# Turning gathered token rows by DMA instead of on the matmul engine, in a graph network with a mixture of experts on one core

## What is computed

```python
x = x + gnn(layernorm(x))     # h = silu(x @ W_in.T + b_in), then h + term_1 + ... + term_6,
                              # term_i = mean over edges of term_(i-1), divided by i; then @ W_out.T + b_out
x = x + moe(layernorm(x))     # 3125 tokens x 256
# moe: 8 experts, each token goes to its 2 best, softmax weights
for e in range(E):
    h = gelu(einsum('bsd,dh->bsh', xn, W1[e]) + b1[e], approximate=False)    # 256 -> 512
    y = y + (einsum('bsh,hd->bsd', h, W2[e]) + b2[e]) * w_full[..., e, None]  # 512 -> 256
```

## Time and profile before

| | |
|---|---|
| Three runs | 1204.22, 1207.3, 1209.26 us; median 1207.3 |
| The profiled execution | 1203.97 us, of which the span of the trace is 1202.2 |
| TensorE clock granted, mean over the span | 0.987 of full |
| Busy in the span | PE 95%, DVE 58%, ACT 35%, POOL 19% |
| Graph part, to the last matmul of line 2059 | to about 1004.5 us |
| Expert tiles, first matmul of line 2173 to last of line 2187 | 1006.4 to 1183.7 us |

### The profile page before, as it was taken

How to read it: one execution, slowest core, us unless ns; L and a number is a source line. 1 busy time by engine, 2 the same in 40 slices (tenths; PEclk the granted TensorE clock), 3 DMA queues, 4 the chain that set the end, 5 groups by cost and what they waited for, 6 DMA issues and landing times.

```text
span 1202.2 us, 26290 instructions
## 1 busy us (share of the span) xinstructions
PE 1143.5 (95%) x7856; PEld 810.2 (67%) x7856; DVE 700.4 (58%) x1425; ACT 418.6 (35%) x806; POOL 227.3 (19%) x279
## 2 busy tenths in 40 slices
PE   5798999999999999999999999999999999899993
PEld 3586777776566666666666666666666667799993
DVE  7898999994444433443155433443344586775666
ACT  1676656663100000000022102121122236677682
POOL 2000000000012121112100000000112236567762
PEclk8998999999999999999999999999999999999997
DMA  6111011013344424443334303331224323323377
GB/s 158 57 43 39 27 32 31 26 34 103 87 92 93 90 56 105 102 100 71 66 114 126 100 23 114 97 109 61 33 66 146 119 84 124 91 79 99 116 211 203
DMA packets 77196, 105.98 MB, mean 88 GB/s; under 512 B 13559, under 2 KB 62510, under 8 KB 76988
## 3 DMA queue, kind: packets, MB, share of 16 engines
q1 hardware_dynamic: 63997, 75.26, 21.0%
q0 software_dynamic: 11376, 25.55, 9.4%
q10 hardware_dynamic: 1740, 4.11, 1.4%
HBM read 77.00 MB, written 37.49 MB: 95 GB/s over the span
## 4 chain that ended last, share of the span: by engine, by line
PE 83%; DVE 9%; DMA 2%; issue 2%; ACT 2%; DVEq 1%; ACTq 0%; POOL 0%; SPq 0%; POOLq 0%
PE ps L2005 45%; PE ps L2059 11%; PE ps L1983 7%; PE ps L2173 5%; PE ps L1951 5%; PE ps L2187 5%; DVE v_b L1244 3%; PE ps L1919 1%; DMA h_ring<-h_dram 1%; PE ps L1930 1%; DVE adj L1151 1%; PE ps L2087 1%; PE ps L2107 1%; ACT v_b L1089 1%; DMA adj<-y_dram 0%
## 5 line engine op out<-in xcount | busy, mean ns | idle before, releaser
L2005 PE MATMUL ps<-v_a,adj 125*125 125x512 f16 x1375 | 297.3, 379 | 0.0
L2005 PE MATMUL ps<-v_b,adj 125*125 125x512 f16 x1250 | 270.2, 379 | 1.5 <-DVE v_b L1269 1.5
L2005 PEld LDWEIGHTS ps<-v_a,adj 125*125 (+1 forms) x1375 | 187.6, 136 | 109.0
L2005 PEld LDWEIGHTS ps<-v_b,adj 125*125 x1250 | 170.6, 136 | 100.9 <-issue 2.0
L964 ACT ACTIVATE t_hi<-ps,cinv 125x256 f32<-125x256 f32 x125 | 59.2, 474 | 457.0 <-PE ps L2005 404.0
L1251 DVE SCALAR_TENSOR_TENSOR t_hi<-ps,cinv,t_hi 125x256 f32<-125x256 f32 x125 | 60.3, 483 | 240.7 <-ACT t_hi L964 240.7
L1244 DVE TENSOR_TENSOR v_b<-v_b 125x2560 f16<-125x2560 f16 x125 | 180.2, 1487 | 3.4 <-PE ps L1951 2.9
L2059 PE MATMUL ps<-v_b,adj 125*125 125x512 f16 x625 | 139.8, 380 | 0.3 <-issue 0.3
L939 ACT ACTIVATE adj<-ps 125x625 f32 (+1 forms) x125 | 112.1, 906 | 66.0 <-PE ps L1951 65.0
L1983 PE MATMUL ps<-v_a,adj 125*125 125x512 f16 x500 | 123.4, 378 | 0.0
L2059 PEld LDWEIGHTS ps<-v_b,adj 125*125 125x125 f16 x625 | 83.4, 137 | 46.2 <-issue 0.7
(11 more groups left out here) (282 smaller groups left out, 986.2 us busy)
## 6 DMA issues: line engine op xcount, KB each, us to landing
h_ring<-h_dram SPq DMA_DIRECT2D x125, 125.0 KB
v_a<-L_ffn_W SPq DMA_DIRECT2D x32, 256.0 KB, 3.4
v_b<-L_ffn_W SPq DMA_DIRECT2D x32, 256.0 KB, 3.4
adj<-w_dram SPq DMA_DIRECT2D x16, 512.0 KB, 5.3
adj<-y_dram SPq DMA_DIRECT2D x8, 560.0 KB
w_dram<-w_hi SPq DMA_DIRECT2D x32, 128.0 KB, 1.9
hx_dram<-h_dram POOLq DMA_DIRECT2D x25, 125.0 KB, 2.4
hx_dram<-x POOLq DMA_DIRECT2D x25, 125.0 KB, 3.2
```

Of the source, the lines that this page charges most:

```text
L2005: last = te.matmul(ps[0:NP, u, :], of_tile(adj[0:NP, 0:ADJ], i, u, a * NP, NP), source[:, a, :], start=(a == 0), stop=(a == T - 1))
```

## The change

- The four transposing matmuls of each tile and ACT's copy out of PSUM are gone. SP issues one transposing DMA a tile instead, from `x_g[j % 8]` straight to `xT16[j % 4]`. It waits for the gather and for `hidden(j-4)`, and PE's `hidden(j)` waits for the DMA. A gather waits for the DMA of the tile eight before.
- Tiles 0 and 1 are turned in SP's last loop pass, before that pass stores its row tile (18); they wait until PE has read `vb[:, 0:4, :]` for the last time (`v_read`). Row tiles 19 to 24 are stored after the transfers of tiles 3 and 9 to 13.
- The loads of lots 0 to 2 go from SP to ACT, behind tiles 42, 43 and 44; ACT waits there for the scatters of tiles 0 to 36. SP's `store(0)` comes just after tile 53 is turned, the other stores and loads after tile 55.
- `HH_TILES` becomes 3 to 16 and 47 to 55 (was 6 to 16 and 44 to 55); 23 tiles in both.

```diff
-    HH_TILES = [*range(6, 17), *range(44, FT)]
+    HH_TILES = [*range(3, 17), *range(47, FT)]
-        TURN_AT = (T - 10, T - 5)
+        LOADS_AT = (42, 43, 44)
 (sync, in the last step's body)
+                if m == T - 1:
+                    sp.wait_ge(S["v_read"], 1)
+                    turned(0)
+                    turned(1)
                 if has(6):
                     rows_out(m - 6, (u - 6) % WIN)
+            def turned(j):
+                sp.wait_ge(g_in[j % FU], 16 * (j // FU + 1))
+                need(sp, S["ffn_h"], j - XR + 1)
+                sp.dma_start_transpose(xT16[j % XR], x_g[j % FU]).then_inc(x_turned[j % XR], 16)
-            for w in range(T - 6, T):
-                rows_out(w, w % WIN)
-            sp.wait_ge(S["tok_ps"], 2)
-            sp.wait_ge(S["idx_ok"], 2)
-            landed(0)
-            for n in range(3):
-                for k in range(TOP):
-                    load(n, k)
-            store(0)
+            for j in range(2, FT):
+                turned(j)
+                if j == XR - 1:
+                    rows_out(T - 6, (T - 6) % WIN)
+                if 9 <= j < 9 + WIN:
+                    rows_out(T - WIN + j - 9, j - 9)
+                if j == FT - 3:
+                    store(0)
             store(1)
 (gpsimd, gather)
-                    pool.wait_ge(S["xg_T"], j - FU + 1)
+                    pool.wait_ge(x_turned[(j - FU) % XR], 16 * ((j - FU) // XR + 1))
 (scalar: transposed(j) and its calls go; in between(j))
+                if j == LOADS_AT[0]:
+                    for r in range(FY):
+                        act.wait_ge(y_out[r], scattered(CLASS_TILES[0], r))
+                if j in LOADS_AT:
+                    n = LOADS_AT.index(j)
+                    t0, t1 = LOTS[n]
+                    for k in range(TOP):
+                        for part in HALVES:
+                            act.dma_start(y_in[n][k][part], y_v[k, part, t0:t1, :]).then_inc(yc_in[n], 16)
 (tensor: transposed(j) and its calls go)
-                        if m == T - 1 and a in TURN_AT:
-                            transposed(TURN_AT.index(a))
+                        if m == T - 1 and a == XR - 1:
+                            last.then_inc(S["v_read"], 1)
 (tensor, hidden)
-                    if j < LAG:
-                        pe.wait_ge(S["xgT_ok"], j + 1)
+                    pe.wait_ge(x_turned[j % XR], 16 * (j // XR + 1))
 (tensor, result)
-                if b == 0 and not alone:
-                    pe.wait_ge(S["xgT_ok"], j + LAG + 1)
```

More of the change, by code:

```diff
@@ L397, in gnn_ffn @@
             pool_turn cover_sum cover_ps cover_ok term_ok e_const e_in e_col e_oh e_mm e_acc e_read e_term e_rows
-            xg_T xgT_ok ffn_h gelu_ok hh_ok hs_ok ffn_y y_ok comb_ok""".split()
+            v_read ffn_h gelu_ok hh_ok hs_ok ffn_y y_ok comb_ok""".split()
         S = {n: sem(n) for n in names}
@@ L406, in gnn_ffn @@
         g_in = [sem(f"g_in{r}") for r in range(FU)]
+        x_turned = [sem(f"turned{r}") for r in range(XR)]
         y_out = [sem(f"y_out{r}") for r in range(FY)]
@@ L432, in turned_in @@
             return [w for w in range(T) if turn_slot(w) == m]
-        def turn_bank(j):
-            return 2 if j == 0 else (j - 1) % 2
         def rows_place(w):
@@ L1023, in body @@
                     normalised(m - 5, u, i)
-                if m == T - 1:
-                    transposed(0)
-                    transposed(1)
                 if has(0):
@@ L1046, in root_of @@
                 a.activation(sd2[:, 0:count], ve2[:, 0:count], ACT.Sqrt).then_inc(S["sd_ok"], 1)
[L1048 to L1053, removed]
             def column(row, w):
@@ L1119, in _ @@
                 if j == 0:
-                    transposed(2)
                     transposed_rows(T - 1)
-                if j + LAG < FT:
-                    transposed(j + LAG)
                 between(j)
@@ L1849, in weighted @@
                     done.then_inc(S["comb_ok"], 1)
-            def transposed(j):
-                pass
             def hidden(j, b, e, part):
@@ L1876, in tables_ready @@
                 pass
-            ffn_tiles(dve, FT, FA, LAG, (experts, parts), 1, transposed, hidden, result, between, tables_ready)
+            ffn_tiles(dve, FT, FA, LAG, (experts, parts), 1, hidden, result, between, tables_ready)
             for n in range(3, len(LOTS)):
@@ L2076, in body @@
                     positions(7, POS_AT, planes_a, oh_pos_a, (0, GA), True, True, 0).then_inc(S["tok_ps"], 1)
[L2078 to L2088, removed]
             def transposed_rows(w):
@@ L2195, in _, with ffn_tiles @@
             pe.wait_ge(S["w_in"], 16 * 2 * NE)
-            ffn_tiles(pe, FT, FA, LAG, (parts,), HK, transposed, hidden, result, between, tables_ready, addresses)
-def ffn_tiles(eng, count, second, lag, tables, steps, transposed, hidden, result, between, tables_ready, addresses=None):
+            ffn_tiles(pe, FT, FA, LAG, (parts,), HK, hidden, result, between, tables_ready, addresses)
+def ffn_tiles(eng, count, second, lag, tables, steps, hidden, result, between, tables_ready, addresses=None):
     entries = {0: [load(0, eng) for load in tables]}
@@ L2208, in ffn_tiles @@
                 result(j - lag, b, *entries[j - lag], alone=j >= count)
-            if b == 0 and 0 < j < count - 2:
-                transposed(j + 2)
             if j < count:
                 hidden(j, b, *entries[j])
-            if b == steps - 1 and j == 0:
-                transposed(2)
             if b == 0 and j + 1 < count and j + 1 != second:
```

## The result

Four runs of the changed kernel took 1218.86, 1218.96, 1219.0 and 1227.47 us, median 1218.98, against 1205.76 for the kernel before (four runs, 1203.66 to 1209.26): **ratio 1.0113, 95% interval 1.0092 to 1.0134, slower by 1.1%**. The forecast was 1197 us, with a range from 1190 to 1208. The profiled execution took 1218.96 us.

A forecast was written before the change was run, and what follows sets the result against it. PE was taken to bound the expert stage, ACT second, DVE early. Terms -12.3 - 1 + 1 + 1 + 1 = -10.3 us on the profiled 1203.97 gave 1193.7, or 1197 against the median 1207.3; range 1190 to 1208.

The forecast's parts named there:

- Point 8: Lot loads' burst from 1140 us: gather and transposing DMA, 7 us each, against 15.9 us less POOL's 2.7; stall 1, bounds 0-6.
- Point 1: PE in the expert stage: 56 groups of transposing matmuls at 0.22 us go, gaining 12.3 us; tile 2.87 to 2.65 us.
- the longer figure weighed beside it: The Trainium skill's about 275 ns per PE transposing matmul, against 55 ns by the rows; 61.6 us gain instead of 12.3.
- Points 3 and 4: DVE-paced first tiles: 1.5 us kept, 1 us more gained; tiles 9 to 16: 1 us taken back; each bounds 0 and 2.
- Point 7: Start of the expert stage: tile 0's transposing DMA lands about 1004.7, PE needs it at 1006.0; cover 1.3 us, cost nothing.
- Point 5: ACT behind tiles 42 to 44: four load issues a lot at 496 ns; 1 us of stall, bounds 0 and 2.6.
- Point 6: Transposing DMA in steady state: 3 us to landing, under 2.65 us of queue time a tile, 8 us cover; cost nothing.
- the slower rival: Expert stage: transposing DMAs do not keep the pitch, a tile takes 3.2 us; 1214 to 1247 us; chance 0.12.

The follow-up runs named there:

- e3: Changed kernel with the twelve loads of lots 0 to 2 cut by max_dma_last_dim=256 into packets of about 256 bytes: 1256.0 us, 1.0112.
- e8: Changed kernel with the loads on SP's queue, close together behind tiles 46, 47 and 48: 1250.98 us, 1.0062.
- e11: Changed kernel with the loads of lots 0 to 2 in pieces of at most 1024 bytes: 1250.47 us, 1.0047.
- e1: Changed kernel without the 12 loads of lots 0 to 2: 1243.25 us, 0.9989 of the kernel before.
- e16: Changed kernel without the loads of lots 0 to 2, a second time: 1246.5 us, 1.0012 of the kernel before.
- e5: The changed kernel as it is, run again beside variants on a later chip: 1.0086 of the kernel before.
- e15: The changed kernel as it is, run again in the last group: 1.0077 of the kernel before.
- e4: Kernel before, turning on PE, with only the loads of lots 0 to 2 moved to ACT behind tiles 42 to 44: 1246.56 us, 1.0023.
- e9: Exact copy of the kernel before, run for its profile on a later chip: 1242.02 us, 0.9979.
- e10: Kernel before, turning on PE, with thirty transposing DMAs added for tiles 12 to 41 into an unread buffer: 1246.31 us, 1.0017.
- the spread version: Changed kernel with the loads four tiles apart: on ACT behind tiles 42, 46, 50, 1.0024 and 1.0053; on SP behind 46, 50, 54, 1.0006 and 1.0016.

## Why the prediction was wrong

**Point 8, the burst, is the step that failed.** It held a gather and a transposing DMA of 7 us each, 14 together, against a cover of some 13, and allowed 1 us of stall, at most 6. Measured for tile 48 were 10.0 and 18.2 us, 28.2 together, and PE waited 13.7 us before tiles 47 and 48. I had taken the scatters' 7.0 us, 1 KB pieces on their own queue, for a transfer in 256-byte packets, while the earlier trace rows had the loads' size: 3.84 MB in 924 packets, 4.2 KB each. Whether the size of the packets is what makes the difference stays argued (e3, e8 and e11). And a term was left out: the clock. Behind the two waits PE ran at its lower level for 17 groups of matmuls, which cost some 5 us more.

That the burst together with the turning by DMA is the cause is shown by e1 and e16 against e5 and e15: without the loads the same kernel is 0.65% faster in one group (1.0012 against 1.0077, the intervals apart) and 1.0% across two (0.9989 against 1.0086), and the long waits are gone. e4 shows that the loads so placed cost 0.2% by themselves while PE turns; the loss takes both parts. These runs were not made on the chip of the result; there it is the trace that puts 17.3 us into the five tiles of the burst.

**Point 1, 12.3 us, held in part.** From tile 17 to 41 the change gained 4.1 us in 24 tiles, 0.17 a tile against 0.22 forecast, and PE was busy without a gap from 1120 to 1140 us with four transposing matmuls fewer in each tile. To go by the measured distance of starts, and not by the longer figure weighed beside it, was right. **Points 3 and 4 were too kind**: by tile 17 the change had won 1.5 us and not 4; DVE's waits grew from 5.2 to 6.3 us. **Point 7 was wrong by 1.4 us**: with 5.9 us to landing instead of 3 the cover of 1.3 was gone, and the weights' load ahead in SP's queue was not named: the diff puts the first transposing DMA past the stores, but not past the loads issued before them. **Point 5**, ACT's issues, had 1 us of stall: they took 0.39 us each in the median, and PE's waits for Gelu were 0.9 us in all against 0.7 before, of which 0.3 lie at the loads. So it was within its bounds and near the lower one. **Point 6** held away from the burst: SP was held 1.19 us a transposing DMA, against an assumed bound of 2.65, so the slower rival, DMAs that cannot keep the pitch, did not come: PE's distance in the open stretch was 2.65 us.

**The sign came from a term and not from a rival.** The slower rival had a chance of 0.12 and the wrong mechanism: no limit of rate in each tile, but one collision of five tiles. What the prediction cited from the Trainium skill beside it (Advanced Engine Details and Errata, DGE: Hardware vs Software: worse hardware-made transposes) is not tested by any run here, since none has a software-made transpose.

**What stays open.** On the four later chips the 0.22 us a tile do not show even without loads. The traces say where they went. PE's issue waits, summed over its lines, are 16.8, 21.1 and 17.4 us in the three kernels that turn on PE (e4, e9, e10), and 19.1 to 27.8, mean 23, in the thirteen that turn by DMA; without the loads (e1, e16) they are 24.8 and 27.8. And the clock is lower: over all runs its mean over the span is 0.974 to 0.975 for the kernel before (medians of the four groups) and 0.9705 and 0.969 for e1 and e16. The stage's mean in one trace of each is 0.94 for e9, 0.91 and 0.90 for e1 and e16; by that, an estimate, PE lost 13 us there in e9 and 20 and 22 in e1 and e16. Some 4 to 7 us of issue and 7 to 9 us of clock are about the 12.3 us that the change takes off.

Why PE waits for issue more is not shown. e10 speaks against the traffic as the reason. That PE gets its instructions at a rate of its own, and has less to do meanwhile, would fit; it was only argued. Why these chips' runs wait for issue and the first ones do not was not tried. Nor is it settled what the spread version would take where the kernel before takes 1206 us: the changed kernel's trace there up to tile 41 lets one expect a few us under the kernel before, but none of the sixteen runs was made there. No changed version beat the kernel before beyond its interval.

## What to carry to other kernels

A DMA that replaces work of an engine must be priced where the queues are fullest (here 18.2 us), and not by what it takes in the open; look at its packets beside those of its neighbours, and at what stands ahead of it in its own queue. If bulk loads have slack, spread them before putting a small, urgent transfer in their stretch. A wait of PE can cost twice: here 13.7 us of waits were followed by some 5 us lost at 1.2 GHz, and on the later chips waits of about 1 us in a row were followed by such stretches too. So count the clock beside the waits when an engine gets less to do and the time does not fall.

## What the runs showed of the hardware

- A transposing DMA of 128 x 512 f16 from SBUF to SBUF is some 550 packets of about 241 bytes, holds SP for 1.19 us (median, 3.4 at most), and takes 0.74 us of the 16 engines.

```profile
L673 SPq DMA_TRANSPOSE v_b<-adj x56: 1188/1192/3372, 1003.7 to 1182.5; - x56
```

- Beside bulk loads the transposing DMAs got 48% of the packets and 6% of the bytes.
- Small packets on the loads move the wait to the issuing engine: ACT was held 1.1 us by one issue in the median and 4.7 at most at 256 bytes, 0.8 and 4.0 at 1 KB, and 0.39 and 1.3 at full size.
- The same program took 1206 us in the runs of the result and 1243 to 1245 on four other chips. The whole difference is in the unrolled expert stage: 21 us more of idle time, nearly all of it waits of PE for its own issue, and some 18 us more of busy time at a lower clock, 0.93 against 1.00.
